# A recommendation tower on one core: table picks gathered ahead of the unit loop, first-layer steps spread singly

## The reference, cut to what matters

```python
# ids [512, 40]; 40 tables of 1000 to 125000 rows x 32; bilinear_matrices [780, 32, 32]
e = jnp.stack([tbl_f[ids[:, f]] for f in range(40)], axis=1)          # [512, 40, 32]
iidx, jidx = jnp.triu_indices(40, k=1)                                # 780 pairs
z = jnp.einsum('bpd,pde,bpe->bp', e[:, iidx], bilinear_matrices, e[:, jidx])
h = jnp.concatenate([z, dense_ctx], axis=1)                           # [512, 796]
h = jnp.maximum(h @ W_top1 + b_top1, 0.0)                             # 512 wide
h = jnp.maximum(h @ W_top2 + b_top2, 0.0)                             # 256 wide
y = h @ W_top3                                                        # [512, 1]
```

## Time and profile before

| what | us |
|---|---|
| median of three runs | 188.95 |
| span of the profiled execution | 304.4 |
| TensorE matmuls busy in it | 210.0 |
| VectorE busy | 159.1 |
| GpSimd busy (gathers) | 95.4 |
| ScalarE busy | 29.8 |

### The profile page before, as it was taken

How to read it: one execution, slowest core, us unless ns; L and a number is a source line. 1 busy time by engine, 2 the same in 40 slices (tenths; PEclk the granted TensorE clock), 3 DMA queues, 4 the chain that set the end, 5 groups by cost and what they waited for, 6 DMA issues and landing times.

```text
span 304.4 us, 3703 instructions
## 1 busy us (share of the span) xinstructions
PE 210.0 (69%) x1590; PEld 62.3 (20%) x1590; DVE 159.1 (52%) x156; ACT 29.8 (10%) x30; POOL 95.4 (31%) x101
## 2 busy tenths in 40 slices
PE   8866443212221221106999999999999999999997
PEld 3212100000000000002433322322222223222223
DVE  2752000210000000004999999999969889898630
ACT  2905000000000000005000000000110100000032
POOL 4777777777777777500000000000000000000000
PEclk9995755555555555555999999999999999999999
DMA  7992010000100100003550097000510004300000
GB/s 238 395 411 68 13 14 13 13 13 13 15 13 14 14 13 13 11 0 98 163 155 3 8 309 202 2 0 2 156 54 0 2 0 121 89 0 2 2 0 0
DMA packets 12688, 20.19 MB, mean 66 GB/s; under 512 B 3840, under 2 KB 6784, under 8 KB 12544
## 3 DMA queue, kind: packets, MB, share of 16 engines
q1 hardware_dynamic: 9168, 18.33, 18.7%
q0 software_dynamic: 3072, 1.58, 3.2%
q10 hardware_dynamic: 432, 0.05, 0.1%
HBM read 12.08 MB, written 0.00 MB: 40 GB/s over the span
## 4 chain that ended last, share of the span: by engine, by line
PE 69%; issue 30%; DVE 0%; ACT 0%
PE y_ps L546 20%; PE z_ps L561 16%; PE t_ps L515 16%; PE t_ps L467 6%; PE y_ps L467 5%; PE z_ps L483 3%; PE y_ps L490 3%; PE t_ps L583 1%; DVE prod L398 0%; ACT y L394 0%
## 5 line engine op out<-in xcount | busy, mean ns | idle before, releaser
L449 DVE TENSOR_TENSOR prod<-y_ps,xt 128x1024 f32<-128x1024 f32 x100 | 115.8, 1217 | 8.1 <-PE y_ps L546 7.6
L301 POOL DMA_INDIRECT x_rows<-rows,row x96 | 94.8, 988 | 29.2 <-issue 29.0
L409 DVE TENSOR_SCALAR hot<-hot_id,number 128x2048 bf16<-128x2048 int16 x32 | 23.6, 758 | 120.3 <-remote 74.7
L546 PE MATMUL y_ps<-xt,m_sb 32*128 32x512 f32 x400 | 65.0, 640 | 0.0
L561 PE MATMUL z_ps<-prod,sel 128*32 128x512 f32 x400 | 53.2, 604 | 0.0
L515 PE MATMUL t_ps<-hot,table 128*32 128x512 bf16 x128 | 19.5, 441 | 30.3 <-issue 30.0
L546 PEld LDWEIGHTS y_ps<-xt,m_sb 32*128 32x128 f32 x400 | 22.5, 182 | 40.6 <-issue 29.4
L515 PE MATMUL t_ps<-hot,low 128*32 128x512 bf16 x128 | 20.8, 436 | 13.5 <-issue 13.1
L515 PE MATMUL t_ps<-hot,rest 128*32 128x512 bf16 x128 | 19.8, 437 | 11.9 <-issue 11.7
L467 PE MATMUL t_ps<-z_t,table 128*32 128x512 f32 x160 | 20.5, 593 | 0.0
L483 PE MATMUL z_ps<-hot_id,sel 128*32 128x512 bf16 x30 | 9.5, 427 | 15.5 <-issue 15.5
(11 more groups left out here) (30 smaller groups left out, 70.5 us busy)
## 6 DMA issues: line engine op xcount, KB each, us to landing
xt<-xt SPq DMA_DIRECT2D x20, 192.0 KB, 2.5
xt<-xt SPq DMA_DIRECT2D x20, 128.0 KB, 2.5
hot_id<-hot_ids SPq DMA_DIRECT2D x4, 512.0 KB, 4.2
table<-w SPq DMA_DIRECT2D x1, 1792.0 KB, 8.2
x_rows<-rows,row POOLq DMA_INDIRECT x96
table<-hot_tables SPq DMA_DIRECT2D x2, 640.0 KB
xt<-xt SPq DMA_DIRECT2D x20, 64.0 KB, 2.1
table<-hot_tables SPq DMA_DIRECT2D x2, 512.0 KB
```

Source lines behind the costliest of these rows:

```text
L301: pool.indirect_dma_start(out=x_rows[:, g, c, :], out_offset=None, in_=rows, in_offset=bass.IndirectOffsetOnAxis(ap=row[:, n:n + 1], axis= ...
L409: nc.vector.tensor_scalar(ones(k).rearrange("p f b -> p (f b)"), hot_id[:, o, :], number[:, o, r:r + 1], None, ALU.is_equal).then_inc(hot_ ...
L449: nc.vector.tensor_tensor(prod[:, k % PROD_UNITS, 2 * half:2 * half + 2, :], y_ps[:, 2 * slot:2 * slot + 2, :], partners[half], ALU.mult). ...
L546: last = nc.tensor.matmul(y_ps[:, 2 * slot + place % 2, :], m_sb[rows, k, :], xt[rows, u, :], start=True, stop=True)
```

## The change

**Picks.** All 36 rounds stand ahead of unit 0. The word is put together differently: the upper half is picked into one PSUM bank as before, but the lower half comes from two byte planes (low byte, and second byte times 256, both exact in bf16) that add up in a second bank. ScalarE makes the planes from the table's bytes (`make_planes`), and after the last round of a group writes the two halves of the words to `xt` as bf16 and as uint16 (`rebuild`). VectorE has no splits left. Each group has two banks of its own (`HOT_BANK`), among them those of the units. The picks of the upper half run two rounds ahead of the planes' (`UPPER_LEAD`). ScalarE makes the indicators of rounds 14, 21 and 30; the ring for VectorE's 33 has six places. The warm-up is 14 matmuls; the fills are gone. SP loads all ids and tables first and all matrices after them.

**Blocks.** The first block has two units, the other six have eight (`place_of`). The dense context goes into free rows of block 0 by four DMAs that ScalarE issues behind its copy of that block.

**First layer.** A step is one block and one m and is evacuated by ScalarE each time: 22 steps behind units 4, 6, ... 42, 45, 47, two late steps, four last ones. The first four go to `h1` with the bias, the other 18 to buffers of their own in `hot`, `plane` and `x_rows`, and GpSimd adds them to `h1`, behind its gathers. VectorE has no joins. `w1` is loaded behind the partner copies of groups 0 and 1 (`HEAD_AFTER` = 2).

**Output layer.** `w3` becomes 32 weight columns (one used), the matmuls have 128 columns each in four row groups of the output, and the result leaves as four rows of 128.

The core of the diff:

```diff
-WARM = 24
-FILL = 4
-SPLIT_FILL = 7
-HOT_RING = 4
+WARM = 14
+HOT_RING = 6
+UPPER_LEAD = 2
-BY_SCALAR = {5: 0, 9: 0, 14: 8, 20: 16}
+BY_SCALAR = {14: 0, 21: 1, 30: 2}
+HOT_BANK = [(0, 1), (2, 3), (4, 5), (6, 7)]
-HEAD_AFTER = 4
+HEAD_AFTER = 2
...
+LATE_BLOCK = BLOCKS - 2
+LATE_PARTS = (2, 3)
+L1_STEP = [(b, m) for b in range(BLOCKS - 1) for m in range(M1) if b < LATE_BLOCK or m not in LATE_PARTS]
 AFTER = {
-    "l1": [18, 24, 26, 27, 28, 28, 31, 32, 33, 34, 36, 37, 41, 41, 43, 44, 46, 47, 48, 49],
+    "l1": [4, 6, 8, 10, 12, 14, 16, 18, 20, 22, 24, 26, 28, 30, 32, 34, 36, 38, 40, 42, 45, 47],
     "turn": [0, 8, 18, 24, 32, 38],
...
+            for n, (b, m) in enumerate(L1_STEP):
+                if b > 0:
+                    pool.wait_ge(t_out, n + 1)
+                    if b > 1:
+                        pool.wait_ge(joined, L1_STEP.index((b - 1, m)) - M1 + 1)
+                    nc.gpsimd.tensor_tensor(h1[:, m, :], part_sb[b][:, m * BATCH:(m + 1) * BATCH], h1[:, m, :],
+                                            ALU.add).then_inc(joined, 1)
...
+            def make_planes(o):
+
+                pieces = 2 if o == 0 else 1
+                n = HOT_ROWS[o] * DIM // pieces
+                act.wait_ge(table_in[o], 16)
+                if o >= PIECE_RING:
+                    act.wait_ge(hot_used, picked(o - PIECE_RING))
+                for piece in range(pieces):
+                    cols = slice(piece * n, (piece + 1) * n)
+                    for byte in (1, 0):
+                        nc.scalar.activation(plane[:, o % PIECE_RING, byte, :, cols], low_byte(table[:, o, :, :], byte)[:, :, cols],
+                                             ACT.Copy, scale=256.0 if byte else 1.0).then_inc(plane_done[o], 1)
...
+            def rebuild(o):
+
+                words = xt[:, HOT_POS[o], :]
+                act.wait_ge(hot_used, picked(o))
+                nc.scalar.activation(halves(words, BF16)[:, :, 1], hot_bank(o, 0), ACT.Copy).then_inc(x_out, 1)
+                nc.scalar.activation(halves(words, U16)[:, :, 0], hot_bank(o, 1), ACT.Copy).then_inc(x_out, 1)
+
+            make_planes(0)
+            make_planes(1)
+            make_ones(scalar_rounds[0])
+            rebuild(0)
+            make_planes(2)
+            make_ones(scalar_rounds[1])
+            rebuild(1)
+            make_planes(3)
+            make_ones(scalar_rounds[2])
+            rebuild(2)
+            rebuild(3)
...
+                    if k == 0:
+                        act.wait_ge(z_out, 1)
+                        for q in range(G):
+                            act.dma_start(z_t[(q + 1) * DIM - G:(q + 1) * DIM, 0, :],
+                                          dense[q * G:(q + 1) * G, :]).then_inc(dense_there, 16)
...
+            for j in range(len(ROUND) + UPPER_LEAD):
+                if j < len(ROUND):
+                    o, r = ROUND[j]
+                    if j in BY_SCALAR:
+                        pe.wait_ge(ones_done, scalar_rounds.index(j) + 1)
+                    else:
+                        pe.wait_ge(hot_done, vector_rounds.index(j) + 1)
+                    if r == 0:
+                        pe.wait_ge(table_in[o], 16)
+                    pick(j, upper(table[:, o, :, :]), hot_bank(o, 0), r == 0, r == HOT_ROWS[o] - 1)
+                if j >= UPPER_LEAD:
+                    o, r = ROUND[j - UPPER_LEAD]
+                    if r == 0:
+                        pe.wait_ge(plane_done[o], 2)
+                    if o == 0 and r == HOT_ROWS[0] // 2:
+                        pe.wait_ge(plane_done[o], 4)
+                    pick(j - UPPER_LEAD, plane[:, o % PIECE_RING, 1, :, :], hot_bank(o, 1), r == 0, False)
+                    pick(j - UPPER_LEAD, plane[:, o % PIECE_RING, 0, :, :], hot_bank(o, 1), False,
+                         r == HOT_ROWS[o] - 1).then_inc(hot_used, 1)
...
+                if what == "l1":
+                    b, m = L1_STEP[k]
+                    if k == 0:
+                        pe.wait_ge(w1_in, 16)
+                        pe.wait_ge(x_out, 2 * HOTS)
+                        pe.wait_ge(dense_there, 16 * G)
                     else:
+                        pe.wait_ge(t_out, k)
                     pe.wait_ge(z_out, b + 1)
+                    by_columns(t_ps[:], w1_sb[:, b, m * P:(m + 1) * P], z_t[:, b, :], True, True).then_inc(part_done, 1)
...
-                for bt in range(BT):
-                    last = nc.tensor.matmul(t_ps[:, bt:bt + 1], h2[:, c, bt * P:(bt + 1) * P], w3_sb[:, c:c + 1],
-                                            start=(c == 0 and bt == 0), stop=(c == M2 - 1), skip_group_check=True)
+                for q in range(QUARTERS):
+                    last = nc.tensor.matmul(t_ps[q * DIM:(q + 1) * DIM, 0:P], w3_sb[:, c, :], h2[:, c, q * P:(q + 1) * P],
+                                            start=(c == 0), stop=(c == M2 - 1), skip_group_check=True)
```

More of the change, by code:

```diff
@@ L123, in schedule @@
             steps.append(("sum", k - LAG))
-            b, r = divmod(k - LAG, PER_BLOCK)
+            b, r = place_of(k - LAG)
             if k - LAG == last_unit(b):
                 steps.append(("z", b))
-        for what in ("fill", "hot", "l1"):
-            steps += [(what, n) for n, after in enumerate(AFTER[what]) if after == k]
-    return steps
[L132 to L147, removed]
@@ L150, in ones_count, with first_round @@
-def ones_count(k, by_scalar):
-    return len([j for j in range(k + 1) if (j in BY_SCALAR) == by_scalar])
-def picked(o):
[L157 to L164, removed]
+        steps += [("l1", n) for n, after in enumerate(AFTER["l1"]) if after == k]
+    return steps
+def picked(o):
+    return sum(HOT_ROWS[:o + 1])
+def first_round(o):
+    return sum(HOT_ROWS[:o])
@@ L167, in bass_dlrm_tower @@
 def bass_dlrm_tower(nc, ids, rows, hot_ids, numbers, negatives, hot_tables, dense, mats, w1, b1, w2, b2, w3, select, out):
     steps = schedule()
[L170 to L181, removed]
@@ L183, in x_there @@
     def x_there(engine, t):
         if t in HOT_POS:
-            fill = fills.index(("hot", picked(HOT_POS.index(t))))
-            engine.wait_ge(t_out, len([s for s in fills[:fill + 1] if not read_by_vector(*s)]))
+            engine.wait_ge(x_out, 2 * HOT_POS.index(t) + 2)
         else:
@@ L248, in upper, with low_byte, halves @@
             return words.bitcast(BF16).rearrange("p f (c two) -> p f c two", two=2)[:, :, :, 1]
+        def low_byte(words, n):
+            return words.bitcast(U8).rearrange("p f (c four) -> p f c four", four=4)[:, :, :, n]
+        def halves(words, dt):
+            return words.bitcast(dt).rearrange("p (b two) -> p b two", two=2)
         y_ps = ps("y_ps", [P, 2 * Y_SLOTS, BATCH])
@@ L281, in bass_dlrm_tower @@
         z_out = sem("z_out")
+        dense_there = sem("dense_there")
         z_last = sem("z_last")
@@ new lines, in pick @@
+            def pick(j, piece, bank, first, last):
+                o, r = ROUND[j]
+                for f in range(G):
+                    done = nc.tensor.matmul(bank[f * DIM:(f + 1) * DIM, :], piece[:, f, r * DIM:(r + 1) * DIM], ones(j)[:, f, :],
+                                            start=first, stop=last, skip_group_check=True)
+                return done
+            for j in range(len(ROUND) + UPPER_LEAD):
+                if j < len(ROUND):
+                    o, r = ROUND[j]
+                    if j in BY_SCALAR:
+                        pe.wait_ge(ones_done, scalar_rounds.index(j) + 1)
+                    else:
+                        pe.wait_ge(hot_done, vector_rounds.index(j) + 1)
[4 more added lines that the diff above has]
+                    o, r = ROUND[j - UPPER_LEAD]
+                    if r == 0:
+                        pe.wait_ge(plane_done[o], 2)
[4 more added lines that the diff above has]
+                         r == HOT_ROWS[o] - 1).then_inc(hot_used, 1)
@@ L526, in _ @@
+            for what, k in steps:
+                if what == "l1":
+                    b, m = L1_STEP[k]
+                    if k == 0:
+                        pe.wait_ge(w1_in, 16)
+                        pe.wait_ge(x_out, 2 * HOTS)
+                        pe.wait_ge(dense_there, 16 * G)
+                    else:
+                        pe.wait_ge(t_out, k)
                     pe.wait_ge(z_out, b + 1)
-                    last = by_columns(t_ps[:], w1_sb[:, b, m * P:(m + 1) * P], z_t[:, b, :],
-                                      b == first, b == end - 1)
```

269 lines of the change are left out of this document (104 added, 165 removed).

## The result

The changed kernel takes 195.7 us (195.3 to 196.0, four runs), the one before 188.9: 1.035 times as long, with an interval of 1.033 to 1.037. The forecast was 188.3, slightly faster. The direction was wrong, and the time lies 3.7 us above the range.

The account below looks back on a forecast made before the run. The opening was taken as bound by VectorE, and the unit stage as paced by VectorE's products and pairs with a step. Forecast: 35.5 + 136.6 + 15.8 + 0.9 = 188.8, less 0.5, so 188.3 us; range 184.8 to 192.0.

Parts of the forecast that it names:

- The opening: Ahead of unit 0: picks end at 35.5 against unit 0 at 30.7 before, 4.8 us later; ScalarE's chain ends at 30.6.
- rival A: Opening: ScalarE's chain is longer than 30.6 us, above all in the planes; total 190.5 or 193 us; chance 0.25.
- the wait for `dense_there`: Unit stage, ahead of step 0: context lands 4.7 us after sum 1, TensorE stands 2.7 us; bounds 0 and 5.
- the clock of the unit stage: No unit-stage loss priced; clock loss was considered in the opening only, taken as 0, upper bound 4.8 us.
- The stage: Unit stage: 133.9 us for units, steps and trailing sums, 136.6 with the dense wait, against 140.15 before.
- The pace of the other pairs: Unit stage: two units with one first-layer step take 5.37 us, so 22 pairs take 118.1.
- 0.9 us between span and run: Whole kernel: 0.9 us unexplained in rebuilding the time before, carried along unchanged.
- late split: Kernel before, ahead of the first product: VectorE's late work adds 1.0 us, absent from the sum after.
- the recurrence: Step-by-step calculation of the two engines; put the stage before 1 us too long, so 0.5 was taken off.
- Rival B: Slow first units hide the dense wait and the function table loads early: 184.6, or 186 with one; chance 0.20.
- C: Unit stage: GpSimd's additions disturb VectorE's products, some 6 us, total 194 us; chance 0.05.
- D: Unit stage not paced by pairs: evenly spread steps hide fully, a unit costs 2.4, total 179 us; chance 0.03.

Follow-up runs that it names:

- the dummies: Changed kernel with dummy matmuls on TensorE behind units 0, 1 and 2 and twelve ahead of the first first-layer step: 195.1 us, ratio 1.032.
- early picks: All 36 indicators made by VectorE, against the changed kernel with all first-layer steps two units later: 185.2 us, ratio 0.981 to the kernel before.
- the one run of 191.1: Fourth run of the changed kernel without the dense context's four loads and their wait: 191.1 us at mean clock 0.97; the other three took 187.9 to 188.6.
- dummies and early picks: Changed kernel with all indicators by VectorE, first-layer steps behind units 28 to 49, and dummy matmuls behind units 0, 1 and 2: 182.8 us, ratio 0.968.

## Why the prediction was wrong

The opening was right: 4.8 us later than before, measured 35.46 - 30.65. ScalarE's chain ended at 30.54 by errors that cancel, which is luck. The function table loaded at 2.15, within the wait for the tables (1.2 less). Against it stand a wait of 0.6 for the second table (9.74), which I did not have, and overlaps worth 0.6 less than the 1.2 that I took off. The bytes cost a column each, as I had them, and the rebuilding copies took 0.73 but followed each other at 0.60. By the 186 ns + 0.833 ns a column of the Trainium skill (ScalarE: Activation LUTs, section What ACT_TABLE_LOAD costs) the ten copies for the planes add up to 9.5 us, an estimate, and not to the 9.9 of the prediction. They measured 9.6 (617, 1054 and 1258 ns each), so the trace agrees. All indicators on VectorE took 3.8 us off: the chain did bind the opening (rival A's place, not its size).

The step that failed is the wait for `dense_there`, the term of 2.7 us. I had the place and the mechanism (step 0 behind unit 4, a load that starts only after a copy) and even named w1 on the same engines, but I priced the landing at the 2.2 us of a load issued at the start and took 5 as the upper bound of the wait. Where first units are not slowed, the wait costs 6.1. The landing hung on the 3.9 MB or so of w1, w2 and partner copies ahead: 17.0 to 17.2 us behind the picks' end in three kernels, whenever the loads were issued. From the end of sum 1 it took 7.4 us with the dummies and 7.9 with early picks (40.72 to 48.59), for my 4.7. In the changed kernel itself it took 5.0 and the stand was 3.14, close to my 4.7 and 2.7. That closeness is luck, since sum 1 came about 3 us late.

Beside it the clock of the unit stage was a term that I put at nothing, having looked for clock losses in the opening only. In the first units of the profiled execution it cost those 2.95 us, and behind the stand 1.2 more. The first loss and the long landing cover the same time: take away only the low clock and 0.6 us are gained, take away only the wait and 4.6 (by the one run of 191.1), take away both and it is 7.7.

The stage again, by its terms: forecast 136.6, measured 142.4 (177.86 - 35.46). Step 0 late by 6.1 for 2.7, 3.4 more; the clock behind it 1.2 more; the rest of the stage 1.2 more, as the kernel without the wait shows (186.2 - 35.3 - 15.8 = 135.1 for my 133.9). Transposes were not quite free: in that kernel three of the five fell into pairs of 5.94, 5.53 and 5.53 us, 0.9 in all. The pace of the other pairs, the second large term, was exact.

The bookkeeping was off by 1.4: I had 0.9 us between span and run and 1.0 for a late split. The split cost 0.1, so that all of the 1.8 is the distance of span and run and stays after the change; and the 0.5 taken off for the recurrence was not there. 188.3 + 5.8 + 0.9 + 0.5 = 195.5, the time of the profiled run. Without its wait my sum gives 185.6 where 188.0 were measured; that the kernel without the wait came out near my 188.3 is luck.

Rival B hoped that slow first units would hide this wait. They did hide half of it, but only by being as late themselves. The step then started at 52.88, and at 53.33 where they were not slow. A did not come: the chain ended where I had it. C fell: the products took 1216 ns in the median beside additions and beside gathers. By the Trainium skill (SBUF — State Buffer, section Who interferes with whom) a VectorE instruction with one SBUF input, outside the two-port modes, does not contend with GpSimd; the trace after agrees. D fell: pairs stayed at 5.37. But its neighbour was there to be had: the price of a step depends on whether its neighbours have one. In every unit a step costs 2.92 - 2.28 = 0.64, in every second 5.37 - 4.56 = 0.81. For 22 steps that makes 3.7 us, of which the two profiled executions show 2.1. The trace of before held both patterns, and I used one. There, two units with a step each start 2.93 apart:

```profile
234.42 1.14 PE L546 MATMUL y_ps<-xt,m_sb 32*128 32x512 f32 x8
...
237.35 1.14 PE L546 MATMUL y_ps<-xt,m_sb 32*128 32x512 f32 x8
```

What stays open: why the clock falls at 40 us in some executions and not in others of the same kernel. In the changed kernel the profiled execution shows it; the other three have a mean clock of 0.98, as has the profiled execution with the dummies, where the first units kept theirs, so the mean doesn't tell. In four of the profiled executions, the changed kernel's not among them, the clock also fell once among the picks, behind TensorE's wait at round 21. With the steps two units later the window reads:

```profile
24.00:26.00 2.00, 2.00 (x24) 0.86 (x20) 1.16 (x2) 2.00 (x3) 1.65 (x2) 0.50 0.24 53
```

The picks ended there at 35.33, as early as without that fall, and at 35.9 to 36.1 in the other three. With dummies and early picks no run lost the clock.

## What to carry to other kernels

A small load that a wait depends on costs what is queued on the DMA engines when it is issued, not what such a load cost on idle engines: look at the DMA share of that stretch and at which large transfers start just before, and ask for the small thing later, or load it first (which no run here tried). A wait on TensorE's queue can cost twice, once for its length and again for the clock behind it: 3.1 and 2.6 us of standing did here, 1.45 did not. Where two delays cover the same time, taking away one gains less than its length, and a forecast needs both. Where the clock holds in some executions of a kernel and not in others, price an edit from executions that are alike in it. When work is spread over a loop that two engines pace, take the price of a spread item and of a bunched one from the trace before choosing.

## What the runs showed of the hardware

Four loads of 8 KB each, issued on ScalarE's queue while 1.8 MB and more from SP's were under way, landed 3.2, 5.2 and 5.9 us after the last issue began, 2 to 3 us after the DMA share had begun to fall from about 1.0; without w1 step 0 started 1.7 us after it. ScalarE's copies of single bytes, four bytes apart, cost 617 ns for 512 columns and 1054 for 1024, where a copy of 512 fp32 columns costs 597. VectorE's int16 indicators ran at 0.67 us for 2048 columns when nothing stopped them. After 3.1 us without a matmul TensorE came back at half clock for about 4 us (0.50 from 54 to 56 us), after 1.45 us it did not (1.00 from 52 to 54 us in the kernel without w1).
